# Normalising the attention heads on GpSimd, after copies on ScalarE, instead of on VectorE

## The reference

```
x = x + attention(layernorm(x));  x = x + moe(layernorm(x))
attention: proj = x @ W_qkv; 32 query heads and 8 key/value heads of 64;
  q, k = rope(q), rope(k); attn = q k^T / 8; masked where q_pos >= k_pos and q_pos < k_pos + 64
  w = softmax([attn, sink]) without the sink's column; out = (w v) @ W_out
moe: 8 experts, top 2 of softmax(x @ gating_w), capacity 640 per expert, relu, weighted sum
```

## Time and profile before

| | us |
|---|---|
| median of 3 runs | 1054.57 (1053.58 to 1058.2) |
| the profiled execution, its time | 1057.24 |
| the profiled execution, span of its instructions | 1055.5 |

### The profile page before, as it was taken

How to read it: one execution, slowest core, us unless ns; L and a number is a source line. 1 busy time by engine, 2 the same in 40 slices (tenths; PEclk the granted TensorE clock), 3 DMA queues, 4 the chain that set the end, 5 groups by cost and what they waited for, 6 DMA issues and landing times.

```text
span 1055.5 us, 32277 instructions
## 1 busy us (share of the span) xinstructions
PE 1024.9 (97%) x12943; PEld 720.9 (68%) x12943; DVE 926.8 (88%) x1967; ACT 655.0 (62%) x1671; POOL 665.1 (63%) x607
## 2 busy tenths in 40 slices
PE   7899999999999999999999999999988999999996
PEld 4466666666666666666666666666656999999995
DVE  6999999999999999999999999999985787777773
ACT  4666667666667766667776666776663555445551
POOL 6667776777666888666787777777752333333332
PEclk9999999999999999999999999999989999999998
DMA  3534544544333334333334334333424555555521
GB/s 112 142 108 118 137 131 140 132 112 135 93 83 83 96 99 111 99 104 81 80 95 114 100 103 121 98 83 96 119 70 162 119 119 123 117 123 124 101 46 21
DMA packets 155893, 112.10 MB, mean 106 GB/s; under 512 B 76480, under 2 KB 145152, under 8 KB 155616
## 3 DMA queue, kind: packets, MB, share of 16 engines
q1 hardware_dynamic: 137680, 90.03, 33.0%
q0 software_dynamic: 7296, 8.55, 4.8%
q10 hardware_dynamic: 10768, 11.46, 3.6%
HBM read 74.84 MB, written 21.83 MB: 92 GB/s over the span
## 4 chain that ended last, share of the span: by engine, by line
PE 56%; DVE 37%; issue 3%; ACT 1%; POOL 1%; DMA 1%; SPq 0%; POOLq 0%; DVEq 0%; ACTq 0%
PE bank L1586 22%; DVE probs_ring L1162 16%; DVE probs_t L1171 14%; PE bank L1562 10%; PE bank L1739 9%; PE bank L1750 6%; DVE heads_sb L1191 4%; PE bank L1753 3%; PE bank L1618 1%; PE bank L1508 1%; PE bank L1526 1%; PE bank L1533 1%; DVE neg_max L1162 0%; ACT probs_ring L862 0%; PE bank L1491 0%
## 5 line engine op out<-in xcount | busy, mean ns | idle before, releaser
L862 ACT ACTIVATE probs_ring<-probs_ring,neg_max 128x512 f32<-128x512 f32 x512 | 365.8, 717 | 210.3 <-DVE neg_max L1162 209.6
L1162 DVE CUSTOM_DVE_ANT_0 probs_ring<-bank,mask,sink_neg 128x512 f32<-128x512 f32 x512 | 360.1, 737 | 26.6 <-PE bank L1562 25.5
L1171 DVE STREAM_TRANSPOSE probs_t<-probs_ring 128x1024 f32<-128x1024 f32 x256 | 317.5, 1240 | 0.2 <-ACT probs_ring L862 0.2
L1562 PE MATMUL bank<-qk_st 64*128 64x512 f32 x1024 | 281.1, 625 | 11.9 <-DVE neg_max L1162 7.4
L1586 PE MATMUL bank<-probs_t,v_quads 32*64 32x256 f32 x8192 | 247.6, 381 | 0.1
L1586 PEld LDWEIGHTS bank<-probs_t,v_quads 32*64 32x64 f32 x8192 | 179.1, 132 | 76.5 <-issue 48.8
L691 POOL TENSOR_TENSOR chunk_sb<-chunk_sb,rope_sb 128x512 f32<-128x512 f32 (+1 forms) x94 | 120.0, 1276 | 103.9 <-issue 82.7
L810 POOL DMA_INDIRECT out<-expert_sb,slots x40 | 78.8, 1969 | 143.1 <-DVE expert_sb L1428 134.5
L1562 PEld LDWEIGHTS bank<-qk_st 64*128 64x128 f32 x1024 | 85.3, 186 | 77.4 <-DVE neg_max L1162 41.8
L696 POOL TENSOR_TENSOR qk_st<-chunk_sb,swap_sb 128x512 f32<-128x512 f32 (+1 forms) x94 | 120.2, 1279 | 7.4
L1618 PEld LDWEIGHTS bank<-wo_sb,heads_sb 64*128 64x128 f32 x992 | 96.1, 187 | 37.4 <-issue 29.2
(11 more groups left out here) (191 smaller groups left out, 1342.7 us busy)
## 6 DMA issues: line engine op xcount, KB each, us to landing
v_quads<-v_rows SPq DMA_DIRECT2D x128, 128.0 KB
recip_wide<-recip_rows SPq DMA_DIRECT2D x64, 256.0 KB
w_raw<-in_L_ffn_w SPq DMA_DIRECT2D x14, 1024.0 KB, 7.6
swap_sb<-chunk_sb SPq DMA_DIRECT2D x314, 32.0 KB
w_raw<-in_L_attn_W_qkv SPq DMA_DIRECT2D x32, 256.0 KB, 2.9
slot_rows<-x2T ACTq DMA_DIRECT2D x8, 662.5 KB, 5.8
slots_cut<-slot_rows SPq DMA_DIRECT2D x56, 80.0 KB, 3.0
w_raw<-in_L_attn_W_qkv SPq DMA_DIRECT2D x64, 64.0 KB, 2.7
```

Source lines behind the costliest of these rows:

```text
L862: nc.scalar.activation(probs[(g * UNITS + n) % RING][:, :], probs[(g * UNITS + n) % RING][:, :], ACT.Exp, bias=neg_max[j][:, n:n + 1], sca ...
L1162: nc.vector.tensor_tensor_reduce(probs[(g * UNITS + n) % RING][:, :], SCORE[SCORE_OF[n // 2][n % 2]][:, :], mask[:, L - P - t * P:2 * L - ...
L1171: nc.vector.transpose(probs_t[j][:, :, (h // 2) * (2 * P):(h // 2 + 1) * (2 * P)] .rearrange("p b (h q) -> p h b q", h=2)[:, :, :, t * BLK ...
L1562: nc.tensor.matmul(SCORE[SCORE_OF[n // 2][hh]][:, :], qk_st[j][half, h // 2, t * P:(t + 1) * P], qk_st[j][half, PAIRS, :], start=True, sto ...
```

## The change

The groups 0 to 30 no longer use DVE for their heads. ACT copies the four PSUM banks into `heads_sb` unscaled (slot 9, after its step of the exponentials), and signals `s_heads_raw` after each two. POOL then scales `heads_sb` in place, in two multiplications of 128x512 (slot 9), and signals `s_heads` after each. Y's first part waits for the first half and, in its middle, for the second. The residual sums, both in slot 6 before, stand apart: odd 1 in slot 4 and odd 0 in slot 9, behind the multiplications. The rotation of Q01 goes from slot 5 to slot 10, behind all of these. Group 31 keeps the operations on DVE.

```diff
-        ROT_AT = {2: Q23, -12: KV, -11: Q01}
+        ROT_AT = {2: Q23, -12: KV, -6: Q01}
...
-        Y_FIRST_OUT_AT, Y_OUT_AT, RESIDUAL_AT = 30, 31, 38
-        ODD_ORDER = (1, 0)
+        Y_FIRST_OUT_AT, Y_OUT_AT = 30, 31
+        RESIDUAL_AT = {36: 1, 41: 0}
...
+                if n == HEADS_AT and g < GROUPS - 1:
+                    pool.wait_ge(s_recip_in, g * 32 + 32)
+                    for half in range(2):
+                        part = slice(2 * half, 2 * half + 2)
+                        pool.wait_ge(s_heads_raw, 2 * g + half + 1)
+                        nc.gpsimd.tensor_tensor(heads_sb[:, part, :], heads_sb[:, part, :], recip_wide[:, part, :],
+                                                ALU.mult).then_inc(s_heads, 1)
+                if n in RESIDUAL_AT and g < GROUPS - 1:
+                    odd = RESIDUAL_AT[n]
+                    i = 1 - odd
+                    pool.wait_ge(s_y_out, 2 * g + i + 1)
...
+                if n == HEADS_AT and g < GROUPS - 1:
+                    act.wait_ge(s_pv, g + 1 + 1)
+                    if later(2 * g):
+                        act.wait_ge(s_y, 2 * g + 1)
+                    for a in range(QUADS):
+                        ins = nc.scalar.activation(heads_sb[:, a, :], PV[a][:, 0:2 * P], ACT.Copy)
+                        if a % 2 == 1:
+                            ins.then_inc(s_heads_raw, 1)
...
-                if n == HEADS_AT:
+                if n == HEADS_AT and g == GROUPS - 1:
                     dve.wait_ge(s_pv, g + 1 + 1)
...
-                    pe.wait_ge(s_heads, 2 * g + (half if g == GROUPS - 1 else 1) + 1 + 1)
+                    pe.wait_ge(s_heads, 2 * g + half + 1 + 1)
...
+                            if half == 0 and second == 1:
+                                pe.wait_ge(s_heads, 2 * g + 1 + 1 + 1)
```

More of the change, by code:

```diff
@@ L186, in moe_layer @@
         s_heads = sem("s_heads")
+        s_heads_raw = sem("s_heads_raw")
         s_y = sem("s_y")
@@ L719, in pool_step @@
                     nc.gpsimd.tensor_tensor(denom[:, :], sums[j][:, :], sink_exp[:, :], ALU.add).then_inc(s_denom, 1)
[L720 to L727, removed]
+                if n == HEADS_AT and g < GROUPS - 1:
[9 more added lines that the diff above has]
+                    pool.wait_ge(s_y_out, 2 * g + i + 1)
+                    if later(2 * g + i):
+                        pool.wait_ge(s_residual, 2 * g + i)
+                    t = (g // NKV) * TPB + odd
+                    nc.gpsimd.tensor_tensor(x_sb[:, t:t + 3:2, :], x_sb[:, t:t + 3:2, :], y_sb[odd][:, :, :],
+                                            ALU.add).then_inc(s_residual, 1)
             roots = [0]
@@ L1184, in dve_step @@
                     nc.vector.transpose(recip_t[:, :], recip[:, :]).then_inc(s_recip, 1)
-                if n == HEADS_AT:
+                if n == HEADS_AT and g == GROUPS - 1:
                     dve.wait_ge(s_pv, g + 1 + 1)
                     dve.wait_ge(s_recip_in, g * 32 + 32)
-                    if later(2 * g):
-                        dve.wait_ge(s_y, 2 * g + 1)
+                    dve.wait_ge(s_y, 2 * g + 1)
                     for a in range(QUADS):
```

## The result

| | us | ratio to before, 95% interval |
|---|---|---|
| before, median of 5 runs beside it | 1055.25 (1053.58 to 1058.2) | |
| after, median of 5 runs | 1126.59 (1125.02 to 1129.32) | 1.0676 (1.0651 to 1.07) |
| predicted | 1112, range 1094 to 1130 | |

The change makes the kernel slower by 6.8%. The profiled execution took 1126.59 us, its instructions span 1124.8; before the span was 1055.5, so 69.3 us have to be found. Reciprocals on DVE (L1197 now) again mark the periods.

What follows compares the result with a forecast made beforehand. A PE-DVE relay was taken to bound the kernel, with POOL's late Q01 rotation then setting S0. Lateness of 50 us plus 8 for the clock on 1057.2 gave 1115, as median 1112; range 1094 to 1130.

Steps and rivals of the forecast that it cites:

- DVE's relief: DVE behind PV's end: 1.42 us of work leaves each period, possible gain 0.45 us, no effect in the longer loop.
- ACT's copies: Four PSUM copies on ACT, about 1.2 us, fit into its 2.63 us idle time; priced at nothing.
- The multiplications: Two 128x512 multiplications on POOL behind PV's end, taken as 2.50 us together.
- Y on time: Y on PE, which waits for the scaled halves, starts about on time; priced at nothing, at most 0.3 us.
- Q01's rotation sets S0: POOL's longer list ahead of this rotation starts S0 0.6 us later; loop 24.5 us instead of 23.9.
- Late k: Periods 7, 8, 24, 25, whose k rotation starts late without scatters: 1.7 to 2.3 us late each, together 8 us.
- Scatters: Eight periods with scatters on POOL now ahead of Q01's rotation: 3.7 to 4.9 us late each, together 33 us.
- The clock: PE drops to 1.2 GHz behind some 4 us idle in eight scatter periods: 1 us each, 8 us.
- The rival that the clock falls in every period: PE's idling before each S0 brings 1.2 GHz in 27 periods: 20 to 35 us more, 1132 to 1147; 6%.
- The signs: Expected profile: S0 or R0 waiting for POOL's `qk_st`, POOL 15% or more of the chain, longer periods, clock below 1.
- ordinary periods: Fifteen periods without late k or scatters: S0 0.5 to 0.9 us late each, together 9 us.
- three periods 0.5: Periods 1, 11 and 27, without residual sums or with DVE work behind the heads, were forecast to break even.

Runs made afterwards that it cites:

- experiment 8: The kernel before the change, with the reciprocal and its transpose on DVE one slot later, behind R2 instead of R1: 1050.35 us, ratio 0.9941.
- experiment 3: The changed kernel without POOL's two multiplications (heads of groups 0 to 30 left unscaled), slot 9's scatters moved behind Q01's rotation: 1054.35 us, ratio 0.9985.
- experiment 2: The changed kernel's POOL order, but heads multiplied on DVE as before, without ACT's copies or POOL's multiplications: 1073.92 us, ratio 1.0161.
- experiment 4: The changed kernel with residual sum odd 0 and the scatters in slot 11, behind Q01's rotation: 1082.98 us, ratio 1.0265.
- experiment 6: The changed kernel with three extra matmuls, result unread, on PE ahead of S0's wait in the eight scatter periods: 1116.94 us, ratio 1.0587.
- experiment 1: The changed kernel with the scatters of slot 9 moved to slot 10, behind Q01's rotation: 1098.03 us, ratio 1.0392.
- experiment 7: The changed kernel with each batch's last pair of scatters moved from slot 9 to slot 3 of the same period: 1114.95 us, ratio 1.0561.
- experiment 5: The changed kernel with Q01's rotation back in slot 5, ahead of the multiplications: 1192.1 us, ratio 1.1281.

## Why the prediction was right, and where it was not

The forecast was 1112, the result 1126.6, inside the range (to 1130) and on the predicted side. The mechanism is the one forecast; some sizes were off, one step was wrong and one place was missing. That the range held in spite of the missing place is in part luck: 6.7 us at the end of the attention stand in no term of it, and the result lies 3.4 below its upper end. Of the 14.6 us that the forecast is short, 11.3 are in the span (58 forecast, 69.3 measured). Another 2.7 were taken off because the profiled execution of the kernel before lay that much above its median, while that of the changed kernel is the median itself; the rest is rounding. The terms named for the range add up to 1091 to 1131 and not to 1094 to 1130, which changes nothing.

**DVE's relief: wrong.** "The possible gain is 0.45 us a period" took DVE's heads, 4% of the chain, for time that PE waits. The chain crosses from PE to DVE at 441.34 because R10 begins behind the heads; but S10, S12, Y and S0 on PE follow one another, with other matmuls between them, without a gap (the rows have no idle time before them), and PE is next held up by DVE before S4, by some 0.2 us (experiment 8). In experiment 3 the value is 0, in three periods 0.55. It did no harm here, as the sum already took it at nothing.

**ACT's copies: right**, at nothing (experiment 3). **The multiplications: right**, 2.54 for two, 2.50 predicted. **Y on time: right.**

**Q01's rotation sets S0: right, 0.2 too small.** The multiplications start 0.91 behind PV's end, where I had 0.68: ACT takes 0.11 to begin and POOL 0.14 from the second copy's end, and I had counted next to nothing for both. R0 comes 1.16 behind S0 instead of 1.06, and PV ends 0.09 sooner. The loop is 24.71 rather than 24.5. Over 15 periods this and period 16 (2.5 longer, 1.6 of it since it starts at the low clock) make 14.1 where 9 were forecast. That it is the multiplications, and not the order alone, experiments 2 and 4 show.

**Late k: right**, 7.4 for 8: in periods 7, 8, 24 and 25 Q01 is ready 12.6 us behind the start of the k rotation, as the sum had it. **Scatters: right**, 33.5 for 33 with the clock taken out (experiment 6); that the scatters stand there, experiment 1.

**The clock: near.** 8 us predicted; experiment 6 gives 5.6 + 1.6 = 7.2 in the eight periods and period 16, and 9.7 by the medians, which contain the start. From S0 to the next mark pass 4.62 us in period 13 and 3.67 in period 17, so the 1 us a fall was right for the place that I had in mind. But part of the loss falls into the next period, whose PV ends up to 1.7 later (14.18 behind the mark in period 16, 12.49 before). The rival that the clock falls in every period is refuted: the granted clock of 240 to 246 us, around a wait of 1.33 us, is 1.00 (its row is in the last section), and behind the wait of 0.54 us S0 to S2 takes 2.35 (481.29 to 483.64), near the 2.25 of before. The rival leant on the page "TensorE: Matmul & The Clock Gate" of the Trainium skill, section HAM oscillation, further than it carries: the loop described there waits some 3 to 5 us for its DMA in each iteration. The changed kernel agrees with that as far as it goes: in the 21 periods with waits of 0.5 to 1.3 us the clock stays up, and it falls at all eight waits of 3.0 to 4.1 us. Shorter waits in another kernel are in the last section.

**The end of the attention: missed**, 6.7 us. I priced the scatters only by what stands behind them in the list and not by who needs their data; for the batch's last pair PE does (experiment 7).

**The signs.** POOL with 15% of the page's chain could not be read, since the chain breaks off at 825 us; the wait of S0 for `qk_st`, 43.1 us in 29 places, says it instead. Three others came a little larger than announced: 24.71 us for 24.4 to 24.6 in ordinary periods, 27.9 to 29.5 for 27.5 to 28.5 in those with scatters, and 0.91 for 0.7 to 0.8 from PV's end to the multiplications.

In one sum: ordinary 14.1 + late k 7.4 + scatters 33.5 + their clock 5.6 + three periods 0.5 + end 6.7 + start 1.6 = 69.4, of 69.3 (rounded terms).

## What to carry to other kernels

An engine with a third of its time free can still have the shortest slack of all: before moving work to it, take the one operation on its list that another engine waits for, and count everything that the change puts in front of it, the DMA issues too, and then who needs the data of each DMA so delayed. Work on an engine that shares the chain with a saturated one can be worth nothing if taken away, as here; look at whether the saturated engine's rows have a gap at that place. Where the profile does show such a gap, even 0.2 us before one matmul, a swap of two neighbours in the order may bring what the large change did not (5 us here, experiment 8).

## What the hardware showed that I had not expected

After a wait of 4.07 us PE's granted clock was 0.50 from 370 to 374 us and 1.00 only from 376 on, so that one wait slows S0 to S4 and sometimes the next period's first products. Around the wait of 1.33 us in period 8 (S0 at 241.44) it stayed at 1.00; the window of the changed kernel, columns as above:

```profile
240.00:246.00 6.00, 4.67 (x34) 2.96 (x32) 4.37 (x9) 3.55 (x12) 5.46 (x7) 1.00 0.58 139
```

The length of a wait alone does not tell whether the clock falls. In experiment 5 it fell around waits of 2.5 us, in experiment 2 it stayed up around one of 2.58, and in experiment 7 even around 3.53 and 3.27. The window at the wait of 2.50 that experiment 5 shows, then the wait of 2.58 in experiment 2 and its window:

```profile
516.00:519.00 3.00, 2.73 (x13) 2.19 (x15) 0.40 (x1) 0.12 (x2) 2.66 (x3) 0.50 0.62 179
```

```profile
608.62 1.13 PE L1564 MATMUL bank<-qk_st 64*128 64x512 f32 x4 [2.58 <-POOL qk_st L697]
```

```profile
608.00:612.00 4.00, 3.38 (x22) 2.23 (x24) 2.22 (x5) 2.46 (x8) 3.54 (x6) 1.00 0.26 60
```

What else decides it, no run here shows.

Three matmuls put directly behind Y, at the start of the long wait, 2.84 us of work, kept the clock at 1.00 (experiment 6), and were worth 7 to 10 us over eight waits although PE then still stood 1.29 us.
